# Attention and mixture of experts on one core: score matmuls addressed to the 32 partitions of their head, with q stored once and no zero padding

## The reference

```python
result = (embeddings @ w_qkv).reshape(b, s, 3, 16, 8)      # q, k, v of 16 heads of 8
scores = jnp.einsum('bnqd,bnkd->bnqk', q, k) / jnp.sqrt(jnp.float32(h))
probs = jax.nn.softmax(scores, axis=-1)
ctx = jnp.einsum('bnqk,bnkd->bnqd', probs, v)
...
x = _layernorm(x + attention(x))
x = _layernorm(x + experts(x))      # 16 experts, 8 chosen by a token, and a shared one
```

## Time and profile before

| | |
|---|---|
| median of 3 runs | 787.39 us |
| the profiled execution | 787.02 us |
| its span in the profile | 785.3 us |
| prologue, to the first k block | 37.8 us |
| attention, first k block to its last context copy | 37.8 to 454.7 us |
| TensorE's matmuls, busy | 758.4 us, 97% of the span |
| VectorE, busy | 536.6 us, 68% |
| ScalarE, busy | 426.5 us, 54% |

### The profile page before, as it was taken

The page is one execution under the profiler, slowest core; times in us unless marked ns, Lnnn a source line. Parts: engine busy times, 40 slices in busy tenths (PEclk is TensorE's granted clock), DMA queues, the critical chain, the costliest instruction groups (busy, mean ns, idle before and its releaser), DMA issues. The chain is left out here.

```text
span 785.3 us, 13279 instructions
## 1 busy us (share of the span) xinstructions
PE 758.4 (97%) x3488; PEld 444.5 (57%) x3488; DVE 536.6 (68%) x1130; ACT 426.5 (54%) x824; POOL 264.4 (34%) x282
## 2 busy tenths in 40 slices
PE   3899999999999999999999999999999999999995
PEld 1355555555555555555555466666666666666663
DVE  2988888888888888887888345565647465656433
ACT  1077767776767777768766843343433343434321
POOL 5111101110111011101110155656665665656563
PEclk7899999999999999999999999999999999999998
DMA  5842142322412323214120040505050505050500
GB/s 174 245 128 57 58 115 63 112 77 59 125 47 66 109 63 107 84 45 140 36 63 4 28 191 2 215 15 214 6 223 0 229 0 229 0 229 0 230 1 27
DMA packets 35816, 74.90 MB, mean 95 GB/s; under 512 B 5680, under 2 KB 15024, under 8 KB 31568
## 3 DMA queue, kind: packets, MB, share of 16 engines
q1 hardware_dynamic: 34976, 72.39, 27.6%
q0 software_dynamic: 816, 2.23, 1.1%
HBM read 58.61 MB, written 15.99 MB: 95 GB/s over the span
## 5 line engine op out<-in xcount | busy, mean ns | idle before, releaser
L662 DVE TENSOR_REDUCE maxima<-ps_q 128x1 f32<-128x512 f32 x512 | 320.2, 682 | 73.0 <-PE ps_q L720 71.8
L620 ACT ACTIVATE probs<-ps_k 128x512 f32<-128x512 f32 x512 | 272.1, 602 | 119.9 <-PE ps_k L726 118.6
L726 PE MATMUL ps_k<-q_pad,k_aug 128*128 128x512 f32 x512 | 223.1, 441 | 1.0 <-ACT probs L620 1.0
L720 PE MATMUL ps_q<-k_aug,q_pad 128*128 128x512 f32 x512 | 206.4, 407 | 10.4 <-DMA q_pad<-q_rows 8.7
L943 POOL TENSOR_TENSOR hidden<-gated,weights 128x512 f32<-128x512 f32 x128 | 167.3, 1313 | 124.0 <-DVE gated L1025 107.8
L973 ACT ACTIVATE silu<-ps_gate 128x512 f32<-128x512 f32 x136 | 81.3, 598 | 176.9 <-PE ps_gate L1067 176.6
L726 PEld LDWEIGHTS ps_k<-q_pad,k_aug 128*128 128x128 f32 x512 | 95.4, 188 | 130.0 <-ACT probs L620 95.4
L1025 DVE TENSOR_TENSOR gated<-silu,ps_up 128x512 f32<-128x512 f32 x128 | 86.9, 684 | 107.0 <-PE ps_up L1067 71.6
L1092 PE MATMUL ps_y<-hidden,nets_down 128*128 128x512 f32 x272 | 137.1, 591 | 0.0
L739 PE MATMUL ps_ctx<-probs,v_ones 128*32 128x512 f32 x1024 | 136.4, 605 | 0.1
L720 PEld LDWEIGHTS ps_q<-k_aug,q_pad 128*128 128x128 f32 x512 | 97.6, 191 | 38.7 <-DVE maxima L662 14.9
(11 more groups left out here) (94 smaller groups left out, 545.6 us busy)
## 6 DMA issues: line engine op xcount, KB each, us to landing
weights<-combine_rows SPq DMA_DIRECT2D x32, 1024.0 KB, 7.9
k_aug<-k_rows SPq DMA_DIRECT2D x32, 256.0 KB, 2.8
q_pad<-q_rows SPq DMA_DIRECT2D x128, 64.0 KB, 2.6
q_rows<-qk_high SPq DMA_DIRECT2D x16, 256.0 KB, 2.9
k_rows<-qk_high SPq DMA_DIRECT2D x16, 256.0 KB, 2.9
net_raw<-w_nets POOLq DMA_DIRECT2D x17, 128.0 KB, 3.1
xT_sb<-xT SPq DMA_DIRECT2D x8, 256.0 KB, 2.8
q_rows<-qk_low SPq DMA_DIRECT2D x8, 256.0 KB, 2.8
```

The lines of the kernel that those rows point to most:

```text
L620: act.activation(probs[:, t % 2, h, :], ps_k[SCORE_SLOT[i]][:], ACT.Exp, scale=ATT_SCALE).then_inc(exp_done, 1)
L662: dve.tensor_reduce(maxima[:, parity, i % UNIT:i % UNIT + 1], ps_q[SCORE_SLOT[i % SCORES]][:], AX_X, ALU.max).then_inc(scores_q_used, 1)
L720: return pe.matmul(ps_q[SCORE_SLOT[i]][:], q_pad[:, g, h, t * P:(t + 1) * P], k_aug[:, g, :], start=True, stop=True).then_inc(scores_q, 1)
L726: return pe.matmul(ps_k[SCORE_SLOT[i]][:], k_aug[:, g, t * P:(t + 1) * P], q_pad[:, g, h, :], start=True, stop=True).then_inc(scores_k, 1)
```

## The change

Each score matmul takes only the 32 partitions of its head from both operands, so it is a matmul with 32 rows of contraction on one of four row tiles (32 rows x 128 columns) of the array. q is stored once, as `q_aug` [128, 4 groups, 512], in the layout of `k_aug`. What follows from it: no zero planes, one transfer for the q of a group, no `q_pads_set` and no `heads_loaded`. The order of the q blocks changes as well: `q_head_tile` gives block i the head (i + 2) mod 4 and the tile i / 4, where it was the head i / 4 and the tile i mod 4. So within a step the row tiles come in the order 0, 2, 1, 3, 2, 0, 3, 1 (k0, q0, k1, ...), and the maxima are stored under the new numbers.

```diff
+def q_head_tile(i):
+
+    return (i + 2) % GROUP, i // GROUP % TILES
...
-def slot_loads(g, times):
...
+def slot_loads(times):
+
+    return DMA * 2 * times
...
-        q_pad = sb("q_pad", [P, GROUPS, GROUP, SEQ], F32R)
+        q_aug = sb("q_aug", [P, GROUPS, SEQ], F32R)
...
-                for h in range(GROUP):
-                    sp.dma_start(q_pad[h * ROWS:(h + 1) * ROWS, g, h, :].bitcast(F32),
-                                 q_rows[g * GROUP + h]
-                                 ).then_inc(heads_loaded if first and h > 0 else slot_loaded[g], DMA)
+                sp.dma_start(q_aug[:, g, :].bitcast(F32),
+                             q_rows[g * GROUP:(g + 1) * GROUP].rearrange("h r s -> (h r) s")
+                             ).then_inc(slot_loaded[g], DMA)
...
-            pool.memset(q_pad[:, 1:, :, :].rearrange("p a b c -> p (a b c)").bitcast(F32), 0.0
-                        ).then_inc(q_pads_set, 1)
...
-                dve.tensor_reduce(maxima[:, parity, i % UNIT:i % UNIT + 1], ps_q[SCORE_SLOT[i % SCORES]][:],
+                h, t = q_head_tile(i)
+                dve.tensor_reduce(maxima[:, parity, TILES * h + t:TILES * h + t + 1], ps_q[SCORE_SLOT[i % SCORES]][:],
...
             def score_q(i):
 
-                g, h, t = i // UNIT, i // 4 % 4, i % 4
-                return pe.matmul(ps_q[SCORE_SLOT[i]][:], q_pad[:, g, h, t * P:(t + 1) * P],
-                                 k_aug[:, g, :], start=True, stop=True).then_inc(scores_q, 1)
+                g = i // UNIT
+                h, t = q_head_tile(i)
+                rows = slice(h * ROWS, (h + 1) * ROWS)
+                return pe.matmul(ps_q[SCORE_SLOT[i]][:], q_aug[rows, g, t * P:(t + 1) * P],
+                                 k_aug[rows, g, :], start=True, stop=True).then_inc(scores_q, 1)
 
             def score_k(i):
 
                 g, t, h = i // UNIT, i // 4 % 4, i % 4
-                return pe.matmul(ps_k[SCORE_SLOT[i]][:], k_aug[:, g, t * P:(t + 1) * P], q_pad[:, g, h, :],
+                rows = slice(h * ROWS, (h + 1) * ROWS)
+                return pe.matmul(ps_k[SCORE_SLOT[i]][:], k_aug[rows, g, t * P:(t + 1) * P], q_aug[rows, g, :],
                                  start=True, stop=True).then_inc(scores_k, 1)
...
-                    if i == 4:
-                        pe.wait_ge(heads_loaded, DMA * (GROUP - 1))
```

More of the change, by code:

```diff
@@ L62, in slot_user_before @@
     return j
-def slot_loads(g, times):
-    first_apart = GROUP - 1 if g == 0 else 0
-    return DMA * ((1 + GROUP) * times - first_apart)
+def q_head_tile(i):
+    return (i + 2) % GROUP, i // GROUP % TILES
+def slot_loads(times):
+    return DMA * 2 * times
 def build(nc, x, xT, w_qkv, w_nets, w_downs, gate_wT, expert_bias, out):
@@ L391, in attention @@
         pads_set = sem("pads_set")
-        q_pads_set = sem("q_pads_set")
         v_pads_set = sem("v_pads_set")
@@ L404, in attention @@
         slot_loaded = [sem(f"slot_loaded{g}") for g in range(GROUPS)]
-        heads_loaded = sem("heads_loaded")
         scores_q = sem("scores_q")
@@ L425, in load_xT, with load_slot @@
                 sp.dma_start(xT_sb[:], xT[:, bass.ds(column, SEQ)]).then_inc(xT_loaded, DMA)
-            def load_slot(g, first=False):
+            def load_slot(g):
                 sp.dma_start(k_aug[:, g, :].bitcast(F32),
@@ L462, in spread_shift @@
                     r = h * ROWS + SHIFT_ROW
-                    sp.dma_start(q_pad[r:r + 2, g, h, :].bitcast(F32),
+                    sp.dma_start(q_aug[r:r + 2, g, :].bitcast(F32),
                                  shift_rows[:, h * TILES:(h + 1) * TILES, :].rearrange("c t q -> c (t q)")
@@ L484, in body @@
                     if g == 0 and not last:
-                        sp.wait_ge(slot_loaded[3], slot_loads(3, b + 1))
+                        sp.wait_ge(slot_loaded[3], slot_loads(b + 1))
                         write_rows(b + 1)
@@ L490, in _ @@
             sp.wait_ge(pads_set, 2)
-            sp.dma_start(q_rows[:, SHIFT_ROW:ROWS, :], q_pad[:, 0, 0, :].bitcast(F32)).then_inc(pads_written, DMA)
+            sp.dma_start(q_rows[:, SHIFT_ROW:ROWS, :], q_aug[:, 0, :].bitcast(F32)).then_inc(pads_written, DMA)
             sp.dma_start(k_rows[:, SHIFT_ROW:ROWS, :], k_aug[:, 0, :].bitcast(F32)).then_inc(pads_written, DMA)
@@ L495, in _ @@
             sp.wait_ge(rows_written, 6 * DMA)
-            load_slot(0, first=True)
-            sp.wait_ge(q_pads_set, 1)
+            load_slot(0)
             load_slot(1)
@@ L701, in _ @@
             dve.memset(k_aug[:, 0, :].bitcast(F32), -1.0).then_inc(pads_set, 1)
-            dve.memset(q_pad[:, 0, :, :].rearrange("p b c -> p (b c)").bitcast(F32), 0.0).then_inc(pads_set, 1)
+            dve.memset(q_aug[:, 0, :].bitcast(F32), 0.0).then_inc(pads_set, 1)
             split_qk(0, 0)
@@ L777, in body @@
                                 if (t, h) == (0, 0):
-                                    pe.wait_ge(slot_loaded[g_next], slot_loads(g_next, b + 1 + (g + AHEAD) // GROUPS))
+                                    pe.wait_ge(slot_loaded[g_next], slot_loads(b + 1 + (g + AHEAD) // GROUPS))
                                 over, i = divmod(i + UNIT * AHEAD, SCORES)
@@ L833, in _ @@
             for u in range(AHEAD):
-                pe.wait_ge(slot_loaded[u], slot_loads(u, 1))
+                pe.wait_ge(slot_loaded[u], slot_loads(1))
                 for i in range(UNIT * u, UNIT * (u + 1)):
-                    if i == 4:
-                        pe.wait_ge(heads_loaded, DMA * (GROUP - 1))
                     if i >= 3:
```

## The result

| | us |
|---|---|
| median before, 4 runs | 787.42 |
| median after, 4 runs (760.73 to 762.9) | 762.52 |
| ratio, 95% interval | 0.9678 (0.9662 to 0.9695) |
| profiled execution after, its span | 760.73, 759.0 |

The account below looks back on a forecast made before the run. TensorE's issue rate was taken to bound the attention. Seven batches gaining 35.0 us and the last 1.9, less small costs, gave -36: 787.0 to 751 us predicted, range 740 to 782.

Parts of the forecast that it names:

- TensorE's issue rate bounds: Attention before the change: TensorE issues throughout a plain step of 3.04 us, where VectorE needs 2.48 and ScalarE 2.06.
- The chain 2.75 + d: Attention step after the change, through q0, its reduction, q3, value matmuls and next k0: 2.82 us, a plain step gaining 0.22.
- d: Issue distance of two score blocks on different row tiles, k0 to q0: taken as 0.07 us, today 0.23.
- Pieces put in: Attention steps with turned maxima, context or projection inserted: 2.85, 3.3, 3.3 us, gaining 0.31, 0.2, 0.6 each.
- Sum of the middle: Attention batches: 5.0 us gained in each of seven, 35.0, plus 1.9 from the last batch's eight steps with q blocks.
- Its other eight stay on the chain of rows 5 ... +0.4: Last batch's eight steps without q blocks: k blocks don't get faster; four inserted pieces pay partly covered shape changes, +0.4 us.
- At the start ... +0.5: Start of the attention loop: some steps still run at the pace of the reductions, costing 0.5 us.
- +0.2 for the transfer: First unit waits for one transfer of 256 KB instead of 64 KB, 2.8 for 2.6 us to land.
- Rival 4: Clock falls to 1.2 GHz as TensorE waits more: some 925 us if throughout; a fifth of the time cancels the gain; 5%.
- Rivals 1 to 3: Reductions bound, 727 us, 5%; weight loads serial, 778, 12%; row tiles don't overlap, shape changes paid, 812, 8%.

## Why the prediction was right, and where not

It was right in sign and within its range (740 to 782), for the reason given, and it was 11.5 us too low. By its steps:

- **TensorE's issue rate bounds**: right. With the blocks on row tiles a batch fell by 5.9 us.
- **The chain 2.75 + d**: right, 2.73 measured. d was taken as 0.07; k0 to q0 is 0.01. The Trainium skill (TensorE: Matmul & The Clock Gate, Part 3) has starts of four row tiles some 4 ns apart, which the trace agrees with (four starts within 0.02), and 3.07 for the whole, by which d would have been 0.075, an estimate from the page: for the chain the first counts, since only q0 stands in it.
- **Pieces put in**: turned maxima were forecast at 2.85 and are hidden (207.63 to 210.37, 2.74; 2.87 in a batch's second unit, 195.99 to 198.86); a projection 3.3, measured 3.31; context 3.3, measured 3.30 (204.33 to 207.63, where VectorE works on it). The change of shape was priced too low: going in was put at 0.32 from start to start (0.23 and 0.09) and is 0.42, which the waits of the chain cover.
- **Sum of the middle**: -36.9 forecast for 30 units (35.0 and 1.9), -41.3 measured in the 29 from unit 2 to unit 31.
- **"Its other eight stay on the chain of rows 5 ... +0.4"**: this is the step that failed. It took the clock from a stretch in which the same blocks ran on 128 rows. It was +11.6, all but some 0.8 of it by the clock.
- **"At the start ... +0.5"** and +0.2 for the transfer: +3.4, again at 1.2 GHz, against an execution of the kernel before with a short low stretch. The prediction read its clock as full "from the second slice on"; the second digit of the earlier trace rows is 8, and only from the third is it 9.
- **Rival 4** came true in part, at the two ends. Its counterargument was drawn from 32 to 36 us of the prologue, where blocks of 128 rows had the clock at 0.98; it didn't ask whether 32-row blocks would. It also leaned on one execution: with the same code there, the kernel before with 32 rows at the end had 0.50 in these 4 us. Its price, a fifth of the time to use up the gain, was of the right order: some 45 us of the 391 in the loop ran low, and 15 of 41 us were lost.
- Rivals 1 to 3 didn't happen. VectorE is 93% busy, yet a step is a chain of 2.73, not the reductions' 2.48.

With the clock held at the end (128 rows there) the kernel takes 749 to 751 us, near the forecast's 751; the gain in the middle that was larger than thought stands against the slow start. That closeness is luck, and so is part of the change's own: the middle gave 4.4 us more than forecast, the two ends took 13.9 more.

## What to carry to other kernels

Put neighbouring small matmuls on different row tiles and keep 128-row or column-tiled work out from between them: here a block behind a change of shape started 0.42 us after the one before it, and 0.23 without. Before counting on it, look at the stretches where TensorE has little to do: there, full-height matmuls cost nothing extra and kept the clock at 2.4 GHz in the traced executions, where the same matmuls on 32 rows lost it. And read the granted clock of each stretch of the new profile, not its mean: 0.951 for 0.988 hid 15 us. Read more than one execution too, since the low stretches differ between executions of one kernel (17 and 30 us at the end of the change).

## What the runs showed of the hardware that wasn't expected

- The clock can stay low for hundreds of us. With the old q order, TensorE's row is busy 100% from 100 to 370 us at 1.2 GHz and VectorE 56%; the same code at 2.4 GHz has VectorE 89% busy from 383 to 432 us. Busy time of pipelined matmuls said nothing of whether the clock would rise.
- Four k blocks a step on 128 rows held 2.4 GHz and on 32 rows lost it, in otherwise identical code (353.9 and 360.8 us for the last part).
- In the prologue, 81 matmuls in 16 us, nearly all on 32 rows, left the clock at 1.2 GHz.
- What follows a score block in another shape starts 0.42 us after it at 2.4 GHz and 0.72 at 1.2 GHz; among 128-row blocks it is 0.23 and 0.43, and a block on another row tile starts 0.01 behind.
